# Projections one head pair ahead instead of three, and the attention product ahead of the transposes, in a token-pooling, attention and expert layer

## The reference, cut to what matters

```python
y = jnp.einsum('ed,bdn->ben', w1, xp)
y = wd[None, :, 0:1] * y[..., :-2] + wd[None, :, 1:2] * y[..., 1:-1] + wd[None, :, 2:3] * y[..., 2:]
...
sim = jnp.einsum('bhid,bhjd->bhij', q, k)
...
attn = jax.nn.softmax(sim, axis=-1)
out = jnp.einsum('bhij,bhjd->bhid', attn, v)
```

## Time and profile before

| what | us |
|---|---|
| median of 3 runs | 1357.37 (1357.0 to 1360.63) |
| the profiled execution | 1359.58 |
| its span, first to last instruction | 1357.8 |
| TensorE busy | 1199.7 (88%) |
| TensorE weight loads busy | 1002.9 (74%) |
| VectorE busy | 892.8 (66%) |
| ScalarE busy | 731.9 (54%) |
| POOL busy | 407.8 (30%) |

### The profile page before, as it was taken

How to read it: one execution, slowest core, us unless ns; L and a number is a source line. 1 busy time by engine, 2 the same in 40 slices (tenths; PEclk the granted TensorE clock), 3 DMA queues, 4 the chain that set the end, 5 groups by cost and what they waited for, 6 DMA issues and landing times. The chain is left out here.

```text
span 1357.8 us, 23184 instructions
## 1 busy us (share of the span) xinstructions
PE 1199.7 (88%) x7812; PEld 1002.9 (74%) x7812; DVE 892.8 (66%) x2614; ACT 731.9 (54%) x1845; POOL 407.8 (30%) x379
## 2 busy tenths in 40 slices
PE   7999999999958999999999999999984998767663
PEld 6999999999946777777777777777763777555452
DVE  5656566665558888888888888988864878122210
ACT  2444534434346778887777888877872441322210
POOL 5000001300023323234443333441111000688885
PEclk9999999999958999999999999999997998987877
DMA  5000000000000000000000000000002000454542
GB/s 140 28 13 24 12 24 13 24 12 13 1 24 12 1 25 25 25 25 19 13 21 25 25 25 25 19 14 9 14 14 61 24 23 4 110 89 82 93 76 36
DMA packets 91800, 42.94 MB, mean 32 GB/s; under 512 B 31066, under 2 KB 88007, under 8 KB 91687
## 3 DMA queue, kind: packets, MB, share of 16 engines
q1 hardware_dynamic: 67207, 33.49, 9.1%
q0 software_dynamic: 23808, 6.69, 3.8%
q10 hardware_dynamic: 672, 1.31, 0.3%
HBM read 28.22 MB, written 9.65 MB: 28 GB/s over the span
## 5 line engine op out<-in xcount | busy, mean ns | idle before, releaser
L485 PE MATMUL bank<-h1hl,W2hl 128*128 128x376 f32 x1536 | 278.9, 337 | 2.6 <-DVE h1hl L638 2.6
L485 PEld LDWEIGHTS bank<-h1hl,W2hl 128*128 128x128 f32 x1536 | 265.2, 190 | 7.2 <-issue 4.3
L1051 ACT ACTIVATE P<-P,nmax 125x375 f32<-125x375 f32 (+2 forms) x384 | 188.9, 501 | 3.6 <-DVE nmax L1182 3.6
L585 ACT ACTIVATE h<-bank,b2c 128x375 f32<-128x375 f32 x128 | 73.6, 575 | 211.2 <-PE bank L485 211.2
L226 POOL TENSOR_SCALAR cellmax<-grid,csb 125x375 f32<-125x375 f32 x96 | 124.2, 1304 | 207.3 <-DVE csb L219 140.8
L1182 DVE CUSTOM_DVE_ANT_0 P<-bank,nbias 125x375 f32<-125x375 f32 (+2 forms) x384 | 138.9, 410 | 6.0 <-PE bank L888 5.8
L1061 ACT COPY PT<-bank 128x500 f32<-128x500 f32 (+1 forms) x256 | 127.3, 550 | 5.3 <-PE bank L907 3.1
L888 PE MATMUL bank<-QK 64*125 64x375 f32 (+2 forms) x768 | 117.7, 411 | 2.4 <-DVE nmax L1182 2.4
L901 PE MATMUL bank<-ident,P 125*128 125x125 f32 x768 | 111.1, 271 | 5.1 <-ACT P L1051 4.5
L1069 ACT ACTIVATE tap<-bank,qkd 128x375 f32<-128x375 f32 x128 | 68.6, 570 | 82.6 <-PE bank L941 82.5
L1649 ACT ACTIVATE hE<-bank,EB 128x375 f32<-128x375 f32 x64 | 36.7, 574 | 134.3 <-PE bank L1598 131.6
(11 more groups left out here) (209 smaller groups left out, 2304.1 us busy)
## 6 DMA issues: line engine op xcount, KB each, us to landing
X<-in_x_dram SPq DMA_DIRECT2D x31, 375.0 KB
EW<-in_L_ffn_w_dram SPq DMA_DIRECT2D x32, 256.0 KB
token_table<-row SPq DMA_DIRECT2D x16, 210.9 KB
tTall<-tT SPq DMA_DIRECT2D x16, 187.5 KB, 2.5
out_dram<-oS SPq DMA_DIRECT2D x16, 187.5 KB
tTall<-in_L_tok_W_dram ACTq DMA_DIRECT2D x1, 1024.0 KB, 8.8
EB<-in_L_ffn_b_dram SPq DMA_DIRECT2D x16, 62.5 KB
tok<-token_table,ids POOLq DMA_INDIRECT x48
```

The costliest lines, as they stand in the source:

```text
L485: last = nc.tensor.matmul(bank[4 + m % 2][:, :NE], W2hl[:, a, k, m * 128:(m + 1) * 128], h1hl[:, p, b, k], start=(k == 0 and n == 0), stop ...
L1051: nc.scalar.activation(P[:, 2 * r + q, SEG[i]:SEG[i] + w], P[:, 2 * r + q, SEG[i]:SEG[i] + w], ACT.Exp, bias=nmax[:, 2 * r + q, i:i + 1], ...
```

## The change

Projections are made one pair ahead of the scores in place of three: at even h of body b, `next_pair(b, h)` is the pair behind (b, c), so body -1 has one projection, at h = 6 and 7, and body 15 has those of its pairs 1, 2 and 3. `attend` stands ahead of `transpose_probs`. The six cells of batch 2 are made in block one (g = 26 to 29, with `take_cs` at g = 23). `transpose_n2` and `take_n2T` go from h = 4 to h = 7, `split_n2T` from h = 5 to h = 0 of the next body; the transposes of the cumulative sums go from h = 7 to h = 6 and the sigmoid from h = 6 to h = 7 of body -1. Semaphore values follow. The diff, cut to its core:

```diff
+                for k in range(TT_):
+                    cell_max(pool, READY, k)
...
+                    if 27 <= g < 30:
+                        cell_weight(act, 2, 2 * (g - 27))
+                        cell_weight(act, 2, 2 * (g - 27) + 1)
...
+                    if g == 23:
+                        take_cs(dve, 2)
...
+                    if 26 <= g < 29:
+                        cell_overlap(dve, 2, 2 * (g - 26))
+                        cell_overlap(dve, 2, 2 * (g - 26) + 1)
...
+            def weights_ahead(m):
+                return READY < m < B
...
-            def projection_step(b, h):
-                return h + 2 if isinstance(b, int) and b == -1 else h
+            def next_pair(b, h):
+                n = 4 * b + h // 2 + 1
+                return n // 4, n % 4
...
-                            if c == 0:
-                                wait(pe, s_pc, m - 2)
-                            if c == 3:
+                            if c == 2:
+                                wait(pe, s_pc, m - 1)
+                            if c == 1:
                                 wait(pe, s_lm, 2 * (m - 1))
...
                 def pool_tokens(m):
-                    wait(pe, s_xn, m)
+                    wait(pe, s_xh, 2 * m)
                     wait(pe, s_tt, m - 3)
-                    if m == READY + 1:
-                        pe.wait_ge(s_csT, 2)
...
                         if valid(b):
                             scores(b, c, part)
-                        if h == 0 and valid(b):
-                            project_qk(b, 3, u)
                         if (b, h) == (0, 0):
                             pe.wait_ge(s_pad, 4)
-                        p = projection_step(b, h)
-                        if p in (2, 4, 6) and valid(b + 1):
-                            project_qk(b + 1, p // 2 - 1, v_)
-                        m, d = value_step(b, h)
+                        m, d = next_pair(b, h)
+                        if part == 0 and valid(m):
+                            project_qk(m, d, m % 2)
                         if part == 1:
-                            n, e = (m, d - 1) if d else (m - 1, 3)
-                            if valid(n):
-                                transpose_v(n, e)
+                            if valid(b):
+                                transpose_v(b, c)
                             if valid(m):
                                 project_v(m, d, m % 2)
+                        m, d = pair_before(b, c, 2)
+                        if part == 0 and valid(m):
+                            attend(m, d, u if c >= 2 else v_)
                         m, d = pair_before(b, c, 1)
                         if valid(m):
                             transpose_probs(m, d, part)
-                        m, d = pair_before(b, c, 2)
-                        if part == 0 and valid(m):
-                            attend(m, d, u if c >= 2 else v_)
...
-                        if h == 4 and ahead(b + 2):
-                            wait(pe, s_g, LN * (b - 1) + 1)
-                            transpose_n2(pe, b + 2, G2)
-                        if (b, h) == (0, 7):
-                            pe.wait_ge(s_xh, 2 * (READY + 1))
+                        if (b, h) == (0, 6):
+                            pe.wait_ge(s_lnd, LN * READY + 1)
                             transpose_cs(pe, B - HEAD, G2, s_zsum, s_cp)
...
+                        if h == 7 and ahead(b + 2):
+                            if b == 0:
+                                pe.wait_ge(s_csT, 2)
+                            wait(pe, s_tt, b)
+                            transpose_n2(pe, b + 2, G2)
...
-                        if h == 4 and ahead(b + 2):
+                        if h == 7 and ahead(b + 2):
                             take_n2T(act, b + 2, G2)
-                        if (b, h) == (-1, 6):
+                        if (b, h) == (-1, 7):
                             act.wait_ge(s_zl, 16)
...
+                        if h == 0 and ahead(b + 1):
+                            split_n2T(dve, b + 1)
...
-                        if h == 5 and ahead(b + 2):
-                            split_n2T(dve, b + 2)
-                        if (b, h) == (0, 7):
+                        if (b, h) == (0, 6):
                             copy_cs(dve, HEAD, B - HEAD, G2, s_cp)
```

More of the change, by code:

```diff
@@ L867, in pair_before @@
                 return b + (c - back) // 4, (c - back) % 4
-            def value_step(b, h):
-                p = projection_step(b, h)
-                return (b, 3) if p == 1 else (b + 1, (p - 3) // 2) if p < HEADS else (-1, 0)
             PARTS = ((2,), (1, 0))
@@ L1002, in body @@
                             m = b - 2
-                            pe.wait_ge(s_v, min(4 * b + 3, 4 * B))
+                            pe.wait_ge(s_v, min(4 * b + 1, 4 * B))
                             pe.wait_ge(s_lf, 3 * m + 3)
@@ L1029, in body @@
                             pe.wait_ge(s_gp, 4 * (m + 1))
-                            pe.wait_ge(s_xh, cap(2 * (b + 3), 2 * B))
+                            pe.wait_ge(s_g, LN * m + 1)
                             transpose_tokens(row, s_ttp)
@@ L1034, in body @@
                             pe.wait_ge(s_tt, m + 1)
-                            pe.wait_ge(s_v, min(4 * (b + 1) + 2, 4 * B))
+                            pe.wait_ge(s_v, min(4 * b + 4, 4 * B))
                             wait(pe, s_pc, cap(m, B))
@@ L1074, in body @@
                         c, part = h // 2, h % 2
-                        p = projection_step(b, h)
-                        m, d = (b, 3) if p == 0 else (b + 1, p // 2 - 1)
-                        if p in (0, 2, 4, 6) and valid(m):
+                        m, d = next_pair(b, h)
+                        if part == 0 and valid(m):
                             first_tap(m, d, 0)
@@ L1080, in body @@
                         if part == 1:
-                            m, d = value_step(b, h)
-                            n, e = (m, d - 1) if d else (m - 1, 3)
-                            if valid(n):
-                                act.wait_ge(s_vtp, 4 * n + e + 1)
-                                wait(act, s_pv, 4 * (n - 2) + e + 1)
-                                nc.scalar.copy(V[:, n % 2, :, e * 128:(e + 1) * 128],
+                            if valid(b):
+                                act.wait_ge(s_vtp, 4 * b + c + 1)
+                                wait(act, s_pv, 4 * (b - 2) + c + 1)
+                                nc.scalar.copy(V[:, b % 2, :, c * 128:(c + 1) * 128],
                                                G1[:PT_, :NT * 128].rearrange("p (t d) -> p t d", d=128)
@@ L1104, in body @@
                         m, k = (b + 3, h - 3) if h else (b + 2, TT_ - 1)
-                        if h not in (1, 2) and ahead(m):
+                        if h not in (1, 2) and weights_ahead(m):
                             cell_weight(act, m, k)
-                        if h == 4 and ahead(b + 2):
+                        if h == 7 and ahead(b + 2):
                             take_n2T(act, b + 2, G2)
-                        if (b, h) == (-1, 6):
+                        if (b, h) == (-1, 7):
                             act.wait_ge(s_zl, 16)
@@ L1147, in body @@
                             normalise(pool, b + 2)
-                        if h >= 2 and ahead(b + 3):
+                        if h >= 2 and weights_ahead(b + 3):
                             cell_max(pool, b + 3, h - 2)
@@ L1266, in body @@
                             nc.vector.tensor_copy(pTs[:], G1[:E, :N]).then_inc(s_pc, 1)
-                        if h == 1 and ahead(b + 3):
+                        if h == 1 and weights_ahead(b + 3):
                             take_cs(dve, b + 3)
```

1 line of the change is left out of this document (removed).

## The result

The changed kernel takes **1337.06 us** (median of 4 runs, 1336.81 to 1337.11); the kernel before, run beside it, 1358.7 (1357.0 to 1360.63). The ratio is 0.984 with a 95% interval of 0.9823 to 0.9857: about 21.6 us less. The profiled execution took 1337.11, span 1335.4, against 1359.58 and 1357.8; the prediction for its like was 1341.2, and 1339.0 for the median.

The account below looks back on a forecast made before the run. TensorE's order of work was taken to set the steady body, with slack at the ends. Terms -19.0 - 1.7 + 3.8 + 0.2 - 1.7 = -18.4 us took the median from 1357.37 to 1339.0; range 1329 to 1348.

Parts of the forecast that it names:

- The front: Body -1: with one pair projected ahead, pooling of batch 2 starts at 390.56 instead of 409.59, 19.0 us less.
- The case in which the sigmoid's rows come late: Front: rows land only at 389, so the tap copy is 5.5 us late; total 1344.5, chance 0.14.
- Body 0: Rest of body 0: the product fills 1.42 of a 2.44 wait, then tap steps bind; 1.7 us less in all.
- Bodies 1 to 13: Steady bodies: a 0.65 us stall at the head less 0.36 gained, net 0.29 a body, 3.8 us more.
- Gain 0.09, and 0.09 in the second pair by the same count; 0.18 in the fourth: Steady bodies: gains in the third, second and fourth pairs from hiding the precw wait, 0.36 us a body.
- The split's cover: Body head, h = 0: VectorE's 0.54 us split is covered by the pooling matmuls of h = 1, over 4 us.
- Body 14: Body 14: only part of the head's stall, as ScalarE has no cell step there; 0.2 us more.
- The end: Body 15: hidden ScalarE waits save 2.7 us, more projected pairs cost 1.0 at 0.5 each; 1.7 us less.
- VectorE sets the bodies: Bodies 1 to 13: stay at 39.3 us, +0.0 instead of +3.8; total 1335, chance 0.14.
- The case of a covered stall: Steady bodies: head stall covered and waits pay in full, 0.36 us a body; total 1330.5, chance 0.08.
- a gain handed back: 14 body heads: n2 activations and transposes follow each other, 1.6 us each, 22.4 lost; total 1357.4, chance 0.05.
- a slower kernel: 14 body heads: n2 step, split and transposes in full, 2.13 us each, late sigmoid besides; total 1370, chance 0.04.

Follow-up runs that it names:

- the order alone: Kernel before the change, with only attend put ahead of transpose_probs and projections left three pairs ahead: 1338.81 us, ratio 0.9844.
- the n2 step moved: Changed kernel with ScalarE's two n2 activations moved from h = 7 to the end of h = 0, VectorE's n2 split to h = 1: 1323.07 us.
- the added transposes: Kernel at 1323.07 us with n2 transposed twice per body, the extra group at h = 7 (1326.95 us) or at h = 6 (1329.22 us).
- the kernel at 1316.27: Kernel at 1323.07 us with pooled-token statistics moved behind the h = 2 taps and their POOL normalisation behind h = 3's cell step: 1316.27 us.
- the order undone: Changed kernel with attend put back behind transpose_probs: 1351.03 us, ratio 0.994.
- the split alone: Changed kernel with only VectorE's split of n2 moved from h = 0 to h = 1, behind the V taps: 1338.14 us.

## Why the prediction held, point by point

**The front** (-19.0, measured -19.76). The steps came in the order worked out: scores between the projections, the sigmoid without a wait, pooling 0.54 earlier than worked out. The clock did better than assumed. The first scores were put at 1.62, the low clock, and took 1.01: the granted clock was 1.00 up to 381.1, and 0.50 from there to 391.3, in the midst of pooling. In the kernel before it was 0.50 from 378.9 to 413.0. The case in which the sigmoid's rows come late, priced at 1344.5, is refuted: the gap is 0.02. That the cells cost nothing in block one is shown by their return: it costs 4.9, and block one ends where it did.

**Body 0** (-1.7, measured -2.19). The wait of 2.44 became 0.87, and the taps bind behind it, 1.25 at 409.87. That is 7.93 behind the pair's first scores (401.94), where 431.3 less 423.35, 7.95, was worked out. But the 433.32 from which the prediction counted had a cause that it didn't name. This is the kernel before, behind the wait:

```profile
430.10:433.40 3.30, 3.30 (x20) 2.10 (x16) 1.98 (x4) 1.55 (x3) 1.22 (x1) 0.50 0.01 2
```

At this clock the product, the n2 transposes and the scores took 1.89, 0.89 and 1.62, where 1.49, 0.54 and 0.91 are usual: 1.5 of the 2.0. In the kernel after, the clock stays at 1.00 from 391.4 to the body's end. So the size was right since the taps were the right bound, and most of the gain is a fall of the clock that didn't come again.

**Bodies 1 to 13** (+3.8, measured +0.66). The step that failed is "Gain 0.09, and 0.09 in the second pair by the same count; 0.18 in the fourth". The head was near: the first pair is 12.41, 0.72 longer, for a stall worked out as 0.65; and the second is 0.12 shorter, for 0.09. The fourth was to become 0.47 - 0.18 = 0.29 longer and is 0.33 shorter. There the n2 transposes cost 0.32 in place of 0.47, and the order alone takes 0.67 (9.02 to 8.35), for a gap of 0.14 that no row labels: 0.31 is at the gap, the rest in the steps around it. The third pair was to lose 0.47 + 0.09 = 0.56 and lost 0.29: the next scores wait 0.23 for the row maxima, a customer of VectorE that the prediction didn't look at. So the order was undersized at 0.36, where it is 1.10; and the n2 step is worth 1.04, not 0.65, since without it the value transposes come 5.22 behind the body's start (541.01 less 535.79), and not the 5.56 of the kernel before (606.46 less 600.90). Two sizes were too small and offset each other: the right total here is partly luck. Had the order alone been forecast by this method, it would have been 12 us off, as the expectation of that run was. The split's cover was right, though VectorE waits 2.8 there (573.04, kernel before) and not "over 4 us".

**Body 14** (+0.2, measured +0.77): its first pair is 8.45 instead of 7.40, so it has the whole stall. That ScalarE has no cell step there didn't help; with the n2 step moved the pair takes 7.44.

**The end** (-1.7, measured -1.17). Again two sizes: the order alone takes 37.50 to 32.00, 5.5 where 2.7 was put, and two more projected pairs put back 4.34, where "0.5 a pair" gave 1.0. The 2.7 left out two waits of the same body in the kernel before, 2.78 together, neither of which is left with the order alone:

```profile
997.94 0.86 PE L901 MATMUL bank<-ident,P 125*128 125x125 f32 x6 [1.36 <-ACT P L1051]
...
1008.20 0.33 PE L907 MATMUL bank<-ident,precw 125*128 125x125 f32 x1 [1.42 <-DVE precw L1220]
```

The difference of bodies 14 and 15 was a poor price for a projected pair, because body 15's pairs were filled with waits for ScalarE then.

**The rivals.** That VectorE sets the bodies and TensorE's waits are worth nothing is refuted by the order alone and by the added transposes, for the body as a whole; in the third pair of the kernel after it holds, 7.70 with the order and without. The case of a covered stall (1330.5) is refuted by the 0.99. The observation behind the first case, Q and K ready only 0.56 ahead, was sound: once the order is in, VectorE's list decides over the rest, 0.63 a body in the kernel at 1316.27. The cases of a gain handed back (1357.4) and of a slower kernel (1370) had the right place, the head, and too high a price: the order's 1.10 was missing in both.

## What to carry to other kernels

Price a wait by undoing it, or from start to start: a row's idle time starts at the modelled end of the group before, and pipelined groups start before that end, so that each wait here cost 0.06 to 0.17 more than it printed. Read the granted clock beside every stretch that is compared, since a fall that comes in one profile and not in the other looks like a cost or a gain of the change. When a change moves two things, run each alone, since a body that stays the same to 0.02 us can hide 1.1 gained and 1.0 lost, and the loss may be a single operation in front of the wrong neighbour. And where an engine ran a long chain without a gap, moving work within it paid only across a point at which the engine waited anyway.

## What the runs showed of the hardware

The code ahead of block two differs in the cells of batch 2 alone, but its time falls in groups. Block two began at 376.4 to 376.8 in the profiles of five kernels (the one after among them), at 378.2 to 378.4 in two (the one before among them), and at 379.0 to 379.7 in five. The windows of 180 to 192, first in the kernel before, then in the one after:

```profile
180.00:192.00 12.00, 11.39 (x63) 11.13 (x63) 5.89 (x10) 3.71 (x7) 0.00 (x0) 0.86 0.00 0
```

```profile
180.00:192.00 12.00, 11.39 (x72) 11.13 (x71) 7.42 (x12) 3.82 (x8) 0.00 (x0) 1.00 0.00 1
```

TensorE is as busy, 11.39, and does 63 matmuls instead of 72: the granted clock is 0.86 instead of 1.00 in the mean. From 184.4 to 187.6 it is 0.50 in the one, the lower level of 1.2 GHz, with 12 matmuls, and 1.00 in the other, with 20. Both have the same pause of 0.61 ahead of it, from 181.5 to 182.1, with TensorE busy for the rest. It makes most of the 1.6 us between these two. All seven kernels that began block two later have this fall and the other five do not, and code does not decide it: the kernels with the order undone and with the split alone have it, and their block one is that of the kernel after. Four of the five latest have a mean granted clock of 0.94 in the first 60 us besides, against 0.97 in the two shown here; what makes the fifth late is not known. This fits the medians of two kernels that agree in every body, the two with added transposes, which lie 2.3 apart, and it is why differences here were read between the same instructions. Waits in block two show it too. Behind the wait for `precw` in the third pair of body 0 the clock fell in both profiles in which it lasts 2.44, in two of the three in which it lasts 1.53 to 1.55, and in none of the seven in which it lasts 0.86 to 0.88; and a wait of 1.94 at the end was followed by a fall in one kernel and not in the other.
